# A GpSimd power operation for the inverse roots of a two-layer transformer kernel

## What is computed

```python
def _tc_rmsnorm(x, t, gw, gb, bw, bb):
    g = (t @ gw.T + gb)[:, None, :]
    b = (t @ bw.T + bb)[:, None, :]
    inv_rms = jax.lax.rsqrt(jnp.mean(x * x, axis=-1, keepdims=True) + EPS)
    return g * x * inv_rms + b
# layer 0
x1 = x + _attention(_tc_rmsnorm(x, ...g1, b1), Wq, Wk, Wv, Wo)       # norm 1
x0 = x1 + _swiglu(_tc_rmsnorm(x1, ...g2, b2), gate_w, hid_w, out_w)  # norm 2
x = x + x0
# layer 1: masked attention of 16 heads, then
rms = jnp.sqrt(jnp.mean(out * out, axis=-1, keepdims=True) + EPS)    # norm 3
xn = out / rms * rms_scale
x = x + xn * (1.0 + sc) + shift
```

## Time and profile before

| | |
|---|---|
| time, median of 3 runs (lowest, highest) | 1044.79 us (1042.7, 1046.22) |
| span of the profiled execution, first to last instruction | 1041.5 us |
| PE (TensorE matmul) busy | 937.9 us, 90% |
| PEld (TensorE weight load) busy | 774.5 us, 74% |
| DVE (VectorE) busy | 683.6 us, 66% |
| ACT (ScalarE) busy | 514.4 us, 49% |
| POOL (GpSimd) busy | 425.1 us, 41%, 772 instructions |
| mean granted TensorE clock | 0.955 of full speed |

### The profile page before, as it was taken

How to read it: one execution, slowest core, us unless ns; L and a number is a source line. 1 busy time by engine, 2 the same in 40 slices (tenths; PEclk the granted TensorE clock), 3 DMA queues, 4 the chain that set the end, 5 groups by cost and what they waited for, 6 DMA issues and landing times. The chain is left out here.

```text
span 1041.5 us, 25169 instructions
## 1 busy us (share of the span) xinstructions
PE 937.9 (90%) x8188; PEld 774.5 (74%) x8188; DVE 683.6 (66%) x1532; ACT 514.4 (49%) x1066; POOL 425.1 (41%) x772
## 2 busy tenths in 40 slices
PE   3568899999999999999999999999998899898883
PEld 3446688887888887888888888888876667666652
DVE  3477657667667567676676677565577777777751
ACT  2235445545545455455354455454455555556451
POOL 6333343434434434434244344345343444444322
PEclk9769899999999999999999999999999999999886
DMA  6445423322332232223222322433255665666600
GB/s 201 102 103 119 89 62 73 74 63 58 69 79 42 61 88 56 61 63 80 61 57 63 86 70 55 86 74 64 63 131 126 139 149 136 144 136 160 144 25 23
DMA packets 82689, 92.10 MB, mean 88 GB/s; under 512 B 7200, under 2 KB 69440, under 8 KB 82624
## 3 DMA queue, kind: packets, MB, share of 16 engines
q1 hardware_dynamic: 82624, 91.28, 38.4%
HBM read 61.09 MB, written 30.15 MB: 88 GB/s over the span
## 5 line engine op out<-in xcount | busy, mean ns | idle before, releaser
L1083 ACT ACTIVATE E<-s2ps 128x512 f32<-128x512 f32 x384 | 214.6, 596 | 179.5 <-PE s2ps L607 144.6
L882 DVE TENSOR_REDUCE nmax<-s1ps 128x2 f32<-128x512 f32 x256 | 163.7, 681 | 4.7 <-PE s1ps L584 4.0
L526 PE MATMUL work<-xch,Gh 128*128 128x256 f32 x512 | 153.0, 299 | 2.2 <-DVE rest L935 1.6
L527 PE MATMUL work<-xcl,Gh 128*128 128x256 f32 x512 | 145.1, 283 | 0.0
L528 PE MATMUL work<-xch,Gl 128*128 128x256 f32 x512 | 145.0, 283 | 0.0
L1330 POOL TENSOR_TENSOR hl<-hf,hh 128x256 fp32r<-128x256 f32 x128 | 98.7, 771 | 106.8 <-PE acc L528 56.9
L607 PE MATMUL s2ps<-stack 100*128 100x256 bf16 x768 | 131.6, 281 | 10.8 <-DMA stack<-m_scr 10.8
L986 DVE SCALAR_TENSOR_TENSOR th<-th,work 128x256 f32<-128x256 f32 x128 | 53.9, 421 | 131.3 <-ACT th L1101 129.8
L624 PE MATMUL pvps<-E,vaug 128*32 128x256 f32 x1536 | 113.9, 400 | 9.3 <-ACT E L1083 8.4
L526 PEld LDWEIGHTS work<-xch,Gh 128*128 128x128 f32 x512 | 97.7, 191 | 21.7 <-issue 14.8
L1101 ACT ACTIVATE th<-work 128x256 f32<-128x256 f32 x128 | 48.9, 382 | 101.9 <-PE work L528 101.9
(11 more groups left out here) (136 smaller groups left out, 2238.9 us busy)
## 6 DMA issues: line engine op xcount, KB each, us to landing
stack<-scr SPq DMA_DIRECT2D x64, 384.0 KB, 4.4
stack<-scr SPq DMA_DIRECT2D x64, 256.0 KB, 5.2
scr<-qp SPq DMA_DIRECT2D x64, 192.0 KB, 2.3
scr<-kp SPq DMA_DIRECT2D x64, 192.0 KB, 2.3
stack<-scr SPq DMA_DIRECT2D x64, 128.0 KB, 5.6
X<-xT SPq DMA_DIRECT2D x16, 256.0 KB, 4.3
yT<-crm SPq DMA_DIRECT2D x16, 256.0 KB, 5.3
E<-w_ffn SPq DMA_DIRECT2D x2, 1024.0 KB, 6.0
```

What stands on the lines that cost most here:

```text
L526: mm(out, lh, rh, start=first, stop=False, skip_group_check=True)
L527: mm(out, lh, rl, start=False, stop=False, skip_group_check=True)
L882: v.tensor_reduce(nmax[:, g // 4, qh, 2 * (g % 4):2 * (g % 4) + 2], s1ps[u % 2][:, :].rearrange("p (h t) -> p h t", h=2), AX_X, ALU.max, n ...
L1083: a.activation(E[:, u % E_RING, :], s2ps[g % 2 if short else u % 2][:, :], ACT.Exp, scale=SCORE_SCALE).then_inc(exp_done, 2 if short else 1)
```

## The change

The guess and the Newton steps go. VectorE's `rsqrt` keeps its first instruction only, the variance with EPS. GpSimd takes `var` to the power of a tile that holds -0.5, in one TENSOR_TENSOR instruction of 128x2 or 128x4, at the same place in its list. It waits for the release of the PSUM bank, which is also the signal that `var` is written. `diagonals` waits for that one operation. Four small tiles give way to one.

```diff
@@ rsqrt, VectorE @@
                 v.tensor_scalar(var[:, c], bank[:, c], EPS, VAR_TOP, ALU.add, ALU.min).then_inc(free, 1)
-                b, k = st.bank("ms")
-                after(dve, work_free[b], k + 1)
-                v.tensor_scalar(half_var[:, c], var[:, c], -0.5, None, ALU.mult).then_inc(guess_order, 1)
-                v.tensor_scalar(half[:, c].bitcast(I32), var[:, c].bitcast(I32), 1, None,
-                                ALU.logical_shift_right).then_inc(guess_order, 1)
-                after(dve, guess_order, 2 * st.n(3) + 2)
-                v.tensor_scalar(rstd[:, c].bitcast(I32), half[:, c].bitcast(I32), -1.0, RSQRT_MAGIC,
-                                ALU.mult, ALU.add).then_inc(guess_ready, 1)
@@ diagonals, VectorE @@
-                after(dve, newton, NEWTON_OPS * (st.n(3) + 1))
+                after(dve, rstd_ready, st.n(3) + 1)
@@ GpSimd, constants @@
-            p.memset(three_halves[:, :], 1.5)
+            p.memset(power[:, :], -0.5)
@@ GpSimd @@
-            def newton_steps(st):
-
-                done = NEWTON_OPS * st.n(3)
+            def inverse_roots(st):
+
                 c = slice(0 if st.L["N"] == 0 else 2, 4 if st.L["C"] is not None else 2)
-                r, t = rstd[:, c], tmp4[:, c]
-                after(pool, guess_ready, st.n(3) + 1)
-                for i in range(3):
-                    after(pool, newton, done + 4 * i)
-                    p.tensor_tensor(t, r, r, ALU.mult).then_inc(newton, 1)
-                    after(pool, newton, done + 4 * i + 1)
-                    p.tensor_tensor(t, t, half_var[:, c], ALU.mult).then_inc(newton, 1)
-                    after(pool, newton, done + 4 * i + 2)
-                    p.tensor_tensor(t, t, three_halves[:, c], ALU.add).then_inc(newton, 1)
-                    after(pool, newton, done + 4 * i + 3)
-                    p.tensor_tensor(r, r, t, ALU.mult).then_inc(newton, 1)
+                b, k = st.bank("ms")
+                after(pool, work_free[b], k + 1)
+                p.tensor_tensor(rstd[:, c], var[:, c], power[:, c], ALU.pow).then_inc(rstd_ready, 1)
@@ step, GpSimd, slot 5 @@
                         if L["N"] == 0 or L["C"] is not None:
-                            newton_steps(st)
+                            inverse_roots(st)
```

More of the change, by code:

```diff
@@ L68 @@
 ONE_PAIR = 1 + 0x3F80 / 2 ** 23
-RSQRT_MAGIC = float(0x5F3759DF)
-NEWTON_OPS = 12
 BRANCH = B - 1
@@ L268, in build @@
         var = sb("var", [P, 4], F32)
-        half_var = sb("half_var", [P, 4], F32)
-        three_halves = sb("three_halves", [P, 4], F32)
-        half = sb("half", [P, 4], F32)
+        power = sb("power", [P, 4], F32)
         rstd = sb("rstd", [P, 4], F32)
-        tmp4 = sb("tmp4", [P, 4], F32)
         nmax = sb("nmax", [P, 2, TC, 8], F32)
@@ L326, in build @@
         work_free = [sem(f"work_free{i}") for i in range(3)]
-        newton = sem("newton")
-        guess_order, guess_ready = sem("guess_order"), sem("guess_ready")
+        rstd_ready = sem("rstd_ready")
         diag_ready = sem("diag_ready")
```

## The result

| | before | after |
|---|---|---|
| median of 5 runs of each (lowest, highest), us | 1042.7 (1042.11, 1046.22) | 1036.79 (1034.06, 1037.86) |
| ratio, 95% interval | | 0.9932 (0.9913 to 0.995) |
| span of the profiled execution, us | 1041.5 | 1034.9 |
| mean granted TensorE clock | 0.955 | 0.959 |

The change makes the kernel 0.68% faster, some 7.1 us of 1043 (5.2 to 9.1 by the interval; the two medians differ by 5.9). The forecast was 3.9 us.

What follows compares the result with a forecast made beforehand. TensorE bounds the middle of layer 0, no engine fills layer 1's, and latency counts at both ends. Gains of 2.66 + 0.8 + 0 + 0.4 = 3.9 us off 1044.8 gave 1040.9 us, range 1039.0 to 1046.2.

Steps and rivals of the forecast that it cites:

- last root: s=32, at the program's end: everything behind it waits, so the shorter chain gains 3.66 - 1.0 = 2.66 us.
- T: Length of GpSimd's power operation in each root: taken as 1.0 us, with 0.2 and 3.2 for the range.
- first root: s=-3, at the start: weight split starts 0.47 us earlier and a wait of 0.36 goes; gain 0.8 us.
- rival D: At s=-3, the first power is held up, for instance by a code load; 1042.9 with 2 us beyond the room; chance 0.05.
- fourth root: s=0: TensorE's wait of 0.77 us shrinks until the rows of maxima are late; gain 0.4, between 0 and 0.8.
- Second root: s=-2: TensorE idles some 6.5 us for diagonals, but the stack from DRAM and maxima are late instead; gain 0.
- third: Root at s=-1: VectorE leaves its own maxima only after the Newton steps have ended and never waits; gain 0.
- In s=1 VectorE waits too: Step s=1: TensorE reaches the broadcast well behind the diagonals, so the shorter chain gains 0.
- Layer 0: s=2 to 12: diagonals stand behind VectorE's maxima and TensorE, the bound, doesn't wait; gain 0.
- Rival B: Layer 0: a power beyond 3.9 us makes TensorE wait in 12 steps; 1057 at 5 us, 1094 at 8; chance 0.15.
- Layer 1, s=13 to 31: Newton steps end well before TensorE's broadcast, and freed time ends in its wait for rows of maxima; gain 0.
- Rivals A and C: Power about as long as the chain, 1.8 to 3.9 us (0.14); early gain lost to transfer or clock, 1042.1 (0.14).

Runs made afterwards that it cites:

- e6: Changed kernel with VectorE's guess instructions and nine dependent GpSimd operations put back in steps 13 to 32 only; 1040.48 us, ratio 0.9939 to the kernel before.
- e6b: The changed kernel with guess and nine GpSimd operations back in steps 13 to 32, measured once more; 1038.34 us, ratio 0.9959 to the kernel before.
- e7: Changed kernel with 14 small GpSimd operations behind each power in steps -3 to 12, without the guess; 1055.56 us, ratio 1.0097 to the kernel before.
- e3: Changed kernel with nine GpSimd operations behind each power in all steps, diagonals waiting for the power alone; 1036.2 us, ratio 0.9918 to the kernel before.

## Why the prediction was right or wrong

**"2.66 us" for the last root.** The mechanism was right, T was mis-sized: 0.71 instead of 1.0. With it the formula gives 3.66 - 0.71 = 2.95, TensorE's two waits give 2.96 (4.55 and 1.59), and the stretch to the end of the program 3.1 to 3.2.

**"T ... I take 1.0 us."** 0.71 for two columns, 1.02 for four. The estimate worked out from the Trainium skill, "GPSIMD Engine Reference", section 3.1, 0.25, is too low by about three times for two columns and four for four. The bounds of 0.2 and 3.2 held.

**"0.8" for the first root.** 0.86 and 0.79 by the next variance, in the two pairs. Power in the shadow of the split, no code load: rival D did not happen. That this passes through did not hold: with the fourth root 1.2 us should have been there by the variance of s=1, and 0.33 and 0.06 were.

**"Second root ... 0"** and **"third ... 0".** Right, by the step that named what is late next: the stack landed 0.9 us earlier and not 3.7, as the diagonals did. The wait of 6.5 us that looked largest was worth nothing.

**"Gain 0.4, between 0 and 0.8" for the fourth root.** TensorE's wait of 0.77 went in both profiles, and what was next late was what the prediction names, the rows of maxima. Their landing scatters: in the first profile they took all of it back, in the repetition a part.

**"In s=1 VectorE waits too, but TensorE reaches the broadcast well behind the diagonals: 0."** This step failed. In s=1 TensorE waited 0.99 us for diagonals that took 1.73 instead of 0.68, because they ran beside GpSimd's residual. I had reasoned on the order of the lists and not looked at the step's rows; it is the fifth of the five waits of the earlier trace rows. The step gave 1.5 and 1.8 us, of which 1.3 and 1.5 are TensorE's busy time at a higher clock; at one clock the old length costs 1.5 to 2.1 us there. So the start gave 1.85 us in both pairs, where 1.2 were forecast, but out of another step. That the two pairs agree is partly luck: two profiles of one kernel (e6 and e6b) differ by 4.2 us there.

**"Layer 0 ... 0."** Right to 0.1 us over nine steps, and so was the point of 3.9 us from which a longer operation costs time. Rival B was a true mechanism whose condition didn't hold.

**"Layer 1, s=13 to 31 ... Freed time ends in that wait: 0."** This step failed at s=16, 0.95 us. It read one step, s=24, and took it for nineteen, though s=16 still has layer 0's swiglu and so rival B's list: chain, residual, low part, TensorE. There the old chain was already beyond the point at which it costs. Rival B had the mechanism and asked only what happens if the chain grows; the same sentence, asked for a chain that shrinks, gives this gain. For the other steps the profiles show nothing beyond their scatter of 2 us.

**Rivals A and C** ask for less than the forecast, and the gain was more. Of C's mechanism, a gain given back to the clock, the profiles show that in step 1 and in s=31 the length goes with the clock, and not that the gain brings the lower clock. In s=31 it goes with it whatever the chain: 17.4 us at 0.50 in the first profile after and in e6, which has the old length there, 15.1 at 0.77 in e6b, which has it too.

**The sum.** The profiles place 1.85 + 0.95 + 3.1 = 5.9 us. The medians of the first comparison differ by 5.9, and the ratios give 7.1 and 5.6. Against the forecast of 3.9 that is 2.0 more: 0.44 at the end, 0.95 at step 16, 0.65 at the start. In the forecast's own terms the start was 1.2 for the first and the fourth root and 0 for s=1; measured were 0.33 and 0.06 for the former, 1.5 and 1.8 for the latter. That 1.2 lay as near to the start's 1.85 as it did was luck.

**The time and the range.** 1036.8 is 4.1 us below the forecast. The other 2.1 are the starting value: I set the gain against 1044.8, the median of three runs, and the median of five was 1042.7. The 3.3 us between median and span came of two different executions; wherever an execution has both, its time is 1.7 to 1.9 us above its span (1036.79 and 1034.9 after). Over the five comparisons the kernel before had medians of 1042.4 to 1046.7. The range allowed 1.4 us for that scatter at its upper end and none at its lower, which was wrong by itself.

## What to carry to other kernels

Shortening a chain pays at the few places where it ends last, and these are the program's ends and its seams, not the many repetitions: of 36 roots, five moved anything by 0.4 us or more (s=-3, 0, 1, 16 and 32), and the first and the fourth had lost most of it again by s=1. List every wait of the engine that is the bound, down to the 0.8 us one that occurs once, and read the rows of each transition step, since the steps in the middle say nothing of them. Where a slow operation would cost time by a queue behind it, ask the same question backwards: where does it cost that time already.

## What the runs showed of the hardware

- A GpSimd power of 128x2 takes 0.71 us and one of 128x4 1.02, against 0.195 for a multiplication of the same shape: by an estimate from the two, some 0.4 us per instruction and 0.15 a column. The first call of the program is no slower.
- VectorE's operations with two inputs in SBUF and GpSimd's held each other up. The diagonals of 128x512 took 0.68 us alone and 1.73 beside the residual (1.75 in e7), those of 128x256 0.42 and 1.49, and the power 2.75 instead of 0.71 beside the weight split. The Trainium skill, "SBUF — State Buffer", section "Who interferes with whom", states one port pair that the two share under an exclusive lock. This trace agrees: the diagonals of 128x512 end 0.54 us behind the residual in s=1 and 0.55 in e7, those of 128x256 0.28 behind it in s=16 before and in e3, though there they had started 0.08 and 0.47 us behind it. With the chain off GpSimd the diagonals of layer 0 took 0.68 us instead of 0.76, and those of s=15 and s=16 0.41 and 0.42 instead of 1.08 and 1.49.
- With the same instructions, step 1 of e6 kept TensorE busy 36.51 us at a granted clock of 0.87 and that of the kernel after 33.44 at 0.95, and in the last 15 us a matmul of 128x256 took 0.41 us at the lower level (0.50) where before it took 0.28.
